# Attention key scores from 32 rows of the array, in pairs of neighbouring heads

## The reference, cut to what matters

```python
def heads(W):
    return (x @ W).reshape(B, S, NUM_HEADS, D_K).transpose(0, 2, 1, 3)
Q, K, V = (heads(WQ), heads(WK), heads(WV))
score = jnp.einsum('bhqd,bhkd->bhqk', Q, K) / jnp.sqrt(jnp.asarray(D_K, x.dtype))
score = score + mask
score = score - jnp.max(score, axis=-1, keepdims=True)
score = jnp.exp(score)
score = score / jnp.sum(score, axis=-1, keepdims=True)
out = jnp.einsum('bhqk,bhkd->bhqd', score, V)
```

## Time and profile before

| | |
|---|---|
| median of three runs | 658.8 us |
| the profiled execution's own time | 656.35 us |
| span of the profile (first to last instruction) | 654.6 us |
| attention windows w = 0 to 15 in it | 28.4 to 211 us |
| window w = 2 | 50.6 to 60.6 us |
| window w = 5 | 84.0 to 96.4 us |

### The profile page before, as it was taken

How to read it: one execution, slowest core, us unless ns; L and a number is a source line. 1 busy time by engine, 2 the same in 40 slices (tenths; PEclk the granted TensorE clock), 3 DMA queues, 4 the chain that set the end, 5 groups by cost and what they waited for, 6 DMA issues and landing times.

```text
span 654.6 us, 9264 instructions
## 1 busy us (share of the span) xinstructions
PE 583.0 (89%) x3347; PEld 433.0 (66%) x3347; DVE 402.2 (61%) x958; ACT 316.2 (48%) x543; POOL 172.9 (26%) x185
## 2 busy tenths in 40 slices
PE   8889989999998379999649698899999999998997
PEld 3556556556564258787536476688778878786866
DVE  6778788798884511432248986884669556762430
ACT  4756566556665204534216243752575255643351
POOL 6112122452543630000058623611300041001100
PEclk9999999999999579999969798999999999999999
DMA  4773242243110455834111100100000000000000
GB/s 130 223 247 110 77 130 65 82 145 97 55 44 2 137 167 167 263 90 118 41 32 32 30 4 2 34 0 1 1 17 2 1 0 18 1 0 1 18 1 17
DMA packets 44926, 42.51 MB, mean 65 GB/s; under 512 B 4176, under 2 KB 34384, under 8 KB 44880
## 3 DMA queue, kind: packets, MB, share of 16 engines
q1 hardware_dynamic: 42544, 37.44, 18.8%
q0 software_dynamic: 2048, 4.20, 2.2%
q10 hardware_dynamic: 288, 0.28, 0.2%
HBM read 25.12 MB, written 16.78 MB: 64 GB/s over the span
## 4 chain that ended last, share of the span: by engine, by line
PE 66%; DVE 10%; ACT 7%; issue 6%; DMA 5%; POOL 4%; SPq 2%; DVEq 0%; POOLq 0%; ACTq 0%
PE ps L1945 7%; PE ps L1615 6%; PE ps L1898 5%; PE ps L1631 5%; PE ps L1643 5%; PE ps L1967 5%; PE ps L1968 4%; PE ps L1889 4%; PE ps L2048 4%; PE ps L2044 4%; PE ps L2045 4%; PE ps L1971 4%; PE ps L1961 2%; DMA XS<-xs_dram 2%; PE ps L1618 2%
## 5 line engine op out<-in xcount | busy, mean ns | idle before, releaser
L679 ACT ACTIVATE PT<-ps 128x384 f32<-128x384 f32 (+1 forms) x192 | 93.5, 529 | 69.9 <-PE ps L1631 67.5
L1052 DVE TENSOR_REDUCE pm<-ps 128x4 f32<-128x512 f32 x160 | 102.3, 681 | 10.0 <-PE ps L1615 9.4
L1615 PE MATMUL ps<-KP,QS 128*128 128x512 f32 x160 | 71.7, 452 | 7.9 <-DVEq L1045 2.5
L546 POOL TENSOR_SCALAR_AFFINE_SELECT PT<-PT 128x512 f32<-128x512 f32 x64 | 39.9, 636 | 129.1 <-ACT PT L679 129.1
L1631 PE MATMUL ps<-QM,KP 128*128 128x512 f32 (+3 forms) x256 | 69.1, 331 | 1.5 <-DVE QM L1066 1.1
L1631 PEld LDWEIGHTS ps<-QM,KP 128*128 128x128 f32 x256 | 43.8, 189 | 22.8 <-issue 12.6
L796 ACT ACTIVATE HT<-ps,cols 128x640 f32<-128x640 f32 x32 | 25.4, 795 | 54.8 <-PE ps L1889 54.8
L1615 PEld LDWEIGHTS ps<-KP,QS 128*128 128x128 f32 x160 | 29.8, 188 | 27.5 <-DVE pm L1052 11.5
L1414 DVE TENSOR_TENSOR_SCAN zero<-decay,OG 128x512 f32<-128x512 f32 x32 | 44.8, 1400 | 1.1
L1643 PE MATMUL ps<-PT,V 128*32 128x128 f32 (+3 forms) x512 | 44.6, 442 | 0.0
L521 POOL TENSOR_TENSOR rstd<-veps,mhalf 128x4 f32<-128x4 f32 x11 | 12.7, 1157 | 110.7 <-DVE veps L963 110.5
(11 more groups left out here) (300 smaller groups left out, 1309.2 us busy)
## 6 DMA issues: line engine op xcount, KB each, us to landing
qk_dram<-HL SPq DMA_DIRECT2D x24, 256.0 KB, 3.5
W<-in_eW SPq DMA_DIRECT2D x16, 256.0 KB, 3.6
QS<-qk_dram SPq DMA_DIRECT2D x15, 256.0 KB
KP<-qk_dram SPq DMA_DIRECT2D x60, 64.0 KB, 2.4
xs_dram<-zero SPq DMA_DIRECT2D x4, 640.0 KB, 3.5
XS<-xs_dram SPq DMA_DIRECT2D x8, 320.0 KB, 5.0
ys_dram<-zero SPq DMA_DIRECT2D x8, 320.0 KB, 2.9
whole_h_w<-in_h_w SPq DMA_DIRECT2D x2, 1024.0 KB, 9.7
```

Source lines behind the costliest of these rows:

```text
L546: g.affine_select(out=diag, in_=diag, pattern=[[0, 4], [1, P]], compare_op=ALU.is_ge, fill=0.0, base=0, channel_multiplier=-1).then_inc(se ...
L679: act.activation(PT[:, i, a:z], bank[ROWB + n % KEYB][:, 0:z - a], ACT.Exp, scale=float(DK) ** -0.5).then_inc(exp_done, 1)
L1052: v.tensor_reduce(pm[:, t, k, :], bank[n % ROWB].rearrange("p (i n) -> p i n", n=P), AXX, ALU.max).then_inc(row_free[n % ROWB], 1)
L1615: mm = pe.matmul(to, QS[:, G % 2, t * P:(t + 1) * P], KP[:, G % 3, k, :, :].rearrange("p i n -> p (i n)"), start=True, stop=t != k)
```

## The change

The matmul of the key scores takes the 32 rows of its head from `KP` and `QM` in place of all 128. The two heads of a pair (0 and 1, 2 and 3 of a chunk) are issued one behind the other; the row scores and values that stood between them now stand between the pairs.

```diff
@@ key_scores(w, n)
-                    mm = pe.matmul(bank[ROWB + n % KEYB][:, at:at + SEQ - j * P], KP[:, w % 3, j, i, :],
-                                   QM[:, w % 2, j * P:SEQ], start=True, stop=True)
+                    mm = pe.matmul(bank[ROWB + n % KEYB][:, at:at + SEQ - j * P], KP[32 * i:32 * i + 32, w % 3, j, i, :],
+                                   QM[32 * i:32 * i + 32, w % 2, j * P:SEQ], start=True, stop=True)
@@ the loop over w
                 turn_max(w)
                 if w:
                     key_scores(w - 1, 10)
+                    key_scores(w - 1, 11)
                 if rows_next:
                     row_scores(w + 1, 2)
                 if w:
-                    key_scores(w - 1, 11)
                     values(w - 1, 1)
                 if rows_next:
                     row_scores(w + 1, 3)
                 key_scores(w, 0)
+                key_scores(w, 1)
                 if b and g == 1:
                     times_wo(b - 1)
...
                 if rows_next:
                     row_scores(w + 1, 4)
-                key_scores(w, 1)
-                if rows_next:
                     row_scores(w + 1, 5)
                 key_scores(w, 2)
+                key_scores(w, 3)
                 if rows_next:
                     row_scores(w + 1, 6)
-                key_scores(w, 3)
                 if w:
                     values(w - 1, 2)
                     values(w - 1, 3)
                 if rows_next:
                     row_scores(w + 1, 7)
                 key_scores(w, 4)
+                key_scores(w, 5)
                 if rows_next:
                     row_scores(w + 1, 8)
-                key_scores(w, 5)
                 if w:
                     turn_out(w - 1)
                 if rows_next:
...
                     logits(b - 1)
-                key_scores(w, 8)
                 if w + 2 < NW:
                     row_scores(w + 2, 0)
+                key_scores(w, 8)
                 key_scores(w, 9)
```

## The result

The changed kernel takes 674.51 us (median of four runs, 672.65 to 676.48); the kernel before, on the same chip, 658.22 us (655.74 to 662.22). The ratio is 1.0242, with a 95% interval of 1.0182 to 1.0302: 2.4% slower, some 16 us. The profiled execution took 673.91 us, with a span of 672.2 us for 654.6 before.

A forecast was written before the change was run, and what follows sets the result against it. TensorE's own pace was taken to bound the windows with nothing of the sequence before. 10.0 us added to the profiled 656.35 made 666.4; the runs' median lies 2.4 higher, so near 669 us, range 655 to 680.

The forecast's parts named there:

- TensorE's own pace bounds the plain windows: Attention windows with nothing of the sequence before: TensorE, busy all 10.00 us, sets the time; w = 2 grows to 10.9 us.
- the signs that were named: Profile of the changed kernel: some eleven new idle "issue" stretches a window, and VectorE's waits for L1615 growing from 0.6 us.
- Pause in, pause out, uncovered load: Each pair between whole-array matmuls costs TensorE 0.10 us in, 0.09 out and two loads of 0.11: 0.41 beside its stream.
- Overlap of a pair: Key scores: two heads on different rows and banks stream together; 0.92 us a window more if they run in a line.
- The pairs of chunk 2: Pairs (8,9) and (10,11): only partly overlapping, 0.27 us of stream + 0.41 = 0.68 for 0.36, plus 0.32 each.
- the wait for an exponential: TensorE's wait before key score 9, 0.3 us in the kernel before, goes or shrinks.
- Half hidden in the windows with VectorE in the chain: Eight windows where TensorE waits for another engine: work added ahead of the wait is hidden, behind it not; 0.5 us each.
- The sum: All attention windows: 5.4 us from six, 4.0 from eight, 0.6 from windows 0 and 15, together 10.0 us more.
- the forecast's own range: Whole kernel with pause, uncovered loads and overlap, chance 0.58: 662 to 676 us, 662 being half hidden in all windows.
- The granted clock: Rival, chance 0.03: idle rows and pauses lower the attention's clock to 1.2 GHz for a while, up to 8 us a window.
- nothing moves: Stages behind the attention: nothing changes there but their start.

The follow-up runs named there:

- the run without the overlap: The changed kernel with both heads of a pair on the 32 rows of the first, so their streams go in a line: 722.88 us in the median.
- the run with 64 rows: The changed kernel with 64 rows per key score (the other head's 32 are zeros) and pairs of heads 0 and 2, 1 and 3: 669.46 us, ratio 1.0169.
- the 32-row version of the same pairs as there: The changed kernel, still 32 rows per key score, but with pairs of heads 0 and 2, 1 and 3: 671.91 us, ratio 1.0187.

## Why the prediction was right, and where its size was off

The forecast was slower, 669 us in a range of 655 to 680; measured is 674.5. Step by step:

- **TensorE's own pace bounds the plain windows.** Right: they grew with its work, 10.00 to 10.83 us for 10.9 predicted, and the chain stayed on TensorE. Of the signs that were named, nine new stretches of "issue" came for the eleven, and VectorE's wait for L1615 did not grow (0.5 us for 0.6; 0.4 us for L1618 came in beside it).
- **Pause in, pause out, uncovered load.** Right for rows as for columns: 0.09, 0.10 and 0.11 us measured. Pairs of 512 columns +0.29 for two (0.32 predicted), the pair behind the values +0.01 (0.02).
- **Overlap of a pair.** Right: two matmuls in the time of one, and the run without the overlap gives 0.65 to 1.26 us a window for the 0.92.
- **The pairs of chunk 2** were mis-sized, each in its own direction. (10,11) overlaps more than I took: 0.38 us from its first start to the row score behind it, where the terms make 0.48. (8,9) takes 0.58 us (72.41 to 72.99 in window 3), since its second head starts 0.22 us behind its first, at 72.62. That is the wait for an exponential, which I had said would go or shrink: key score 9 needs the bank that the exponential of key score 6 frees, and that one ended at 72.57. It doesn't stand in the list of waits, since the loads of the first head fill the time (the 0.4 us in that list is the pause before pair (2,3)). The sum over the window came out right with two errors in it. The exponential:

```profile
72.08 0.49 ACT L679 ACTIVATE PT<-ps 128x384 f32<-128x384 f32 x1 [1.77 <-PE ps L1631]
```

- **Half hidden in the windows with VectorE in the chain.** Right in size, and by luck: with the clock at 1.00 they grew by 0.70, 0.48, 0.48, 0.11, 0.50, 0.48, 0.55 and 0.47 us (w = 4, 5, 7, 8, 9, 11, 12, 13, the fifth of them, w = 9, by the run with 64 rows) for 0.5 predicted, and the plain ones by 0.63 to 0.84 for 0.9. But I had said that the wait hides what is added ahead of it and not what is added behind. In window 5 it is the other way round. The row score that waits, and VectorE's wait for TensorE, before and then after:

```profile
92.02 0.50 PE L1615 MATMUL ps<-KP,QS 128*128 128x512 f32 x1 [0.89 <-DVE pm L1052]
DVE X L1088 <- PE ps L1677: 0.9, 1, 0.9
```

```profile
96.22 0.50 PE L1615 MATMUL ps<-KP,QS 128*128 128x512 f32 x1 [0.92 <-DVE pm L1052]
DVE X L1088 <- PE ps L1677: 1.5, 1, 1.5
```

The wait is as long as before, and its end has moved from 8.05 to 8.60 us behind the `turn_max` of the window (83.97 and 87.62): 0.55 us, more than the whole growth of 0.48. VectorE's work ahead of that maximum starts from a product of TensorE (`times_wo`, L1677), in front of which two pairs now stand; VectorE waits 0.6 us longer for it, and the chain that ended last in this window now runs from L1677 through `X`. What lies behind the wait has even lost 0.06 us, since key score 5 has moved ahead of it. Windows 9 (with 64 rows) and 13 show the same.
- **The sum.** Windows 0 to 14 sum to 8.6 us more (180.2 for 171.6 us, with 64 rows) for 9.7 in the sum. One bound of the forecast's own range doesn't follow from its words: half hidden in all sixteen windows is 9.7 us and makes 668, not 662.
- **The granted clock** is the step that failed. I gave it 0.03 on the ground that `values` with its pauses hadn't lowered it. It fell in the profiled execution in window 9 (16.28 us for 12.59, 3.7 us) and once more from 216.4 us, in the last window, which in the kernel before was through its key scores (209.6 us) before the clock went down at 215.7; from the last `turn_max` to the last key score it is 12.1 us for 9.6. The mean clock of all four runs (0.943 to 0.953) says that it wasn't this one alone. Against the 64-row version, which beside the rows differs only in which heads make a pair, the changed kernel's ratio is 0.7% higher, some 5 us; against the 32-row version of the same pairs as there, which kept more of its clock, it is 0.5% higher. The price of the clock thus differs from execution to execution.

The Trainium skill's TensorEngine Tiling says in Key Properties that a change of the tiling mode drains TensorE. The traces agree, for rows too: 0.32 us into a pair for 0.23 within the whole array.

The span grew by 17.6 us: 0.3 ahead of window 0, 8.6 for the shape in windows 0 to 14, 3.7 for the clock in window 9, and 5.0 behind the last `turn_max`. Of these 5.0, 2.4 lie in the end of the attention, as above. The rest is in stages that the change doesn't touch, where I had said that nothing moves. The runs with the new order show 0 to 5 us behind the last `turn_max` as well (0.1 with pair (6,7) alone on 32 rows, 1.4 with 128 rows, 4.7 with 64, whose clock held until 226.3 us, behind its key scores), so I don't ascribe it, and it isn't shown that the 2.4 are a net loss either. What exactly makes the clock fall stays open: the rows, the pauses, the waits ahead of them, or several together. Against the 10.0 us that the sum has, the 17.6 of the span are 1.1 less for the shape in windows 0 to 14, 3.7 more in window 9, 4.7 more behind the last `turn_max` and 0.3 ahead of window 0; in medians it is 674.5 us for 669.

## What to carry to other kernels

Small row groups don't come free inside a stream of whole-array matmuls: here each stretch of another shape costs 0.41 us beside its stream, so a pair of 512 columns (0.23 us to gain) loses, a pair beside work that has changed shape already breaks even, and four together win 0.3 us by these terms (0.9 us a window was measured for three such groups). Count the changes of shape in the order of the work before counting what overlaps, and look for the cost on the matmul behind the small one. And check the granted clock of the stretch afterwards, in several executions: it cost 3.7 us in window 9 here, and 8.2 us in one window of the version with 32 rows in the old order (21.00 us for 12.76), in places that the edit doesn't name.

## What the runs showed that I had not expected

The matmuls of a pair don't start in the order of the program. `key_scores` issues 256 and 128 columns of one head, then 256 and 128 of the next. In the changed kernel (two narrow stretches of window w = 3):

```profile
63.26 0.39 PE L1631 MATMUL ps<-QM,KP 32*128 32x256 f32 x2
```

```profile
63.48 0.22 PE L1631 MATMUL ps<-QM,KP 32*128 32x128 f32 x2
```

Both of 256 columns start first, 0.01 us apart, and 0.22 us later both of 128: the second head's first matmul goes ahead of the first head's second, which uses rows that are still at work. In 28 of the 32 such pairs both matmuls of 256 columns start ahead of both of 128. This is why (10,11) was cheaper than a count in program order says. The two loads of a pair, of 128 columns each, also run beside each other, in 0.18 us together (65.27), where two on the whole array follow each other at 0.11 us.

The second surprise is how uneven the clock makes a kernel: the version with 32 rows in the old order ran between 712 and 747 us with the same program and data, while the whole-array version of the new order stayed within 656.64 to 660.77 in ten runs.
